# Moving a ternary quantisation and some norm sums out of a setup stage, with one multiplication given to GpSimd

## The reference

```
x = x + 0.5 * _L0_ffn_ref(_layernorm(x), w_gate_up, w_proj)     # the stage at hand
x = x + _L0_attn_ref(_layernorm(x), w_qkv, w_out)               # 16 heads
x = x + 0.5 * _L0_ffn_ref(_layernorm(x), w_gate_up, w_proj)
x = x + 0.5 * _L1_ffn_ref(...)   # mixture of experts
x = x + _L1_attn_ref(...)        # retention
x = x + 0.5 * _L1_ffn_ref(...)

def ternary_quant(w_fp32, g=64):
    w = w_fp32.astype(bfloat16); w_g = w.reshape(-1, g)
    scale = clip(mean(abs(w_g), axis=-1, keepdims=True), 1e-08, None)
    w_hat = (clip(round(w_g / scale), -1, 1) * scale).reshape(w.shape)
    return w + stop_gradient(w_hat - w)

def _L0_ffn_ref(x, w_gate_up, w_proj):      # w_gate_up [2048, 256], w_proj [256, 1024]
    gate, up = split(x @ ternary_quant(w_gate_up).T, 2)
    h = silu(gate) * up
    return rms_norm(h) @ ternary_quant(w_proj).T
```

## Time and profile before

| | us |
|---|---|
| median of 3 runs | 1762.09 (1761.56 to 1762.62) |
| profiled execution, its own time | 1760.51 |
| its span in the profile | 1758.7 |
| busy in the span: PE, DVE, ACT, POOL | 1645.4, 1287.1, 1219.9, 1126.1 |
| first matmul of the feed-forward stage begins at | 50.85 |

### The profile page before, as it was taken

How to read it: one execution, slowest core, us unless ns; L and a number is a source line. 1 busy time by engine, 2 the same in 40 slices (tenths; PEclk the granted TensorE clock), 3 DMA queues, 4 the chain that set the end, 5 groups by cost and what they waited for, 6 DMA issues and landing times.

```text
span 1758.7 us, 26693 instructions
## 1 busy us (share of the span) xinstructions
PE 1645.4 (94%) x9307; PEld 963.8 (55%) x9307; DVE 1287.1 (73%) x2427; ACT 1219.9 (69%) x1886; POOL 1126.1 (64%) x747
## 2 busy tenths in 40 slices
PE   0898789999999999999999999998999999899998
PEld 0565345555555555555555555554565565676565
DVE  7877657777777777767777777786687778886766
ACT  6655778888888888988988888874654443325432
POOL 0554768888888888888888878883763222653222
PEclk9999899999999999999999999999999999999999
DMA  8100567887888878889878788784001210000001
GB/s 284 49 1 19 101 115 144 139 138 144 150 150 146 147 140 154 148 135 164 144 136 152 130 145 151 128 137 89 0 1 58 64 40 1 1 1 28 28 10 48
DMA packets 580506, 174.03 MB, mean 99 GB/s; under 512 B 543243, under 2 KB 579350, under 8 KB 580246
## 3 DMA queue, kind: packets, MB, share of 16 engines
q1 hardware_dynamic: 580374, 172.33, 51.8%
HBM read 35.94 MB, written 2.10 MB: 22 GB/s over the span
## 4 chain that ended last, share of the span: by engine, by line
PE 73%; DVE 8%; POOL 2%; issue 2%; ACT 1%; SPq 0%; DMA 0%; DVEq 0%; POOLq 0%; ACTq 0%
PE banks L1789 23%; PE banks L1790 23%; PE banks L1791 23%; DVE X L1644 1%; POOL sq_sum L684 1%; DVE mo_h L1631 1%; DVE nmax L1463 1%; DVE x L1196 1%; PE banks L1887 1%; PE banks L1855 1%; PE banks L1888 1%; PE banks L1856 1%; PE banks L1939 0%; PE banks L1799 0%; PE banks L2100 0%
## 5 line engine op out<-in xcount | busy, mean ns | idle before, releaser
L737 POOL TENSOR_TENSOR Pl<-Pm,Ph 128x1024 f16<-128x1024 f32 x256 | 546.4, 2134 | 52.3 <-ACT Ph L962 51.3
L952 ACT ACTIVATE Pm<-banks,nbias,s_scale 128x1024 f32<-128x1024 f32 x256 | 308.0, 1203 | 135.9 <-DVE nbias L1465 135.7
L1463 DVE TENSOR_REDUCE nmax<-banks 128x1 f32<-128x1024 f32 x256 | 312.6, 1221 | 111.6 <-PE banks L1791 110.5
L962 ACT ACTIVATE Ph<-Pm 128x1024 f16<-128x1024 f32 x256 | 268.3, 1048 | 1.2
L716 POOL TENSOR_TENSOR rp_b<-rp_s,rope 128x512 f32<-128x512 f32 x128 | 162.8, 1272 | 150.9 <-ACT rp_s L929 150.9
L1502 DVE SCALAR_TENSOR_TENSOR X<-banks,rinv,X 128x256 f32<-128x256 f32 x256 | 112.7, 479 | 156.8 <-PE banks L1791 156.8
L790 POOL TENSOR_TENSOR mT_lo<-mo_h,mT_hi 128x512 f16<-128x512 f32 x72 | 83.7, 1162 | 214.2 <-ACT mT_hi L1064 213.9
L1789 PE MATMUL banks<-QK_hi 128*128 128x512 f16 x512 | 197.1, 385 | 6.8 <-DVE QK_lo L1539 2.7
L1789 PE MATMUL banks<-PT_hi,V_hi 128*128 128x512 f16 x512 | 194.9, 381 | 3.2 <-DMA PT_lo<-Pl 3.2
L1790 PE MATMUL banks<-QK_lo,QK_hi 128*128 128x512 f16 x512 | 195.5, 382 | 0.0
L1791 PE MATMUL banks<-QK_hi,QK_lo 128*128 128x512 f16 x512 | 195.5, 382 | 0.0
(11 more groups left out here) (240 smaller groups left out, 4136.4 us busy)
## 6 DMA issues: line engine op xcount, KB each, us to landing
moe_raw<-in_L_ffn_W SPq DMA_DIRECT2D x72, 128.0 KB, 2.3
w_all<-in_L_attn_w_qkv SPq DMA_DIRECT2D x3, 2048.0 KB, 16.5
a_raw<-in_L_attn_w_qkv SPq DMA_DIRECT2D x24, 256.0 KB, 3.1
PT_hi<-Ph SPq DMA_TRANSPOSE x256, 3.4
PT_lo<-Pl SPq DMA_TRANSPOSE x256, 3.4
raw_gu<-in_L_ffn_w_gate_up SPq DMA_DIRECT2D x2, 1024.0 KB, 7.3
X<-in_L_attn_x SPq DMA_DIRECT2D x2, 1024.0 KB, 13.1
o_raw<-in_L_attn_w_out SPq DMA_DIRECT2D x8, 256.0 KB, 3.4
```

What stands on the lines that cost most here:

```text
L737: nc.gpsimd.tensor_tensor(Pl[:, z % 4, :], Pm[:, k, :], Ph[:, z % 4, :], ALU.subtract).then_inc(pl_done.sem, 1)
L952: nc.scalar.activation(Pm[:, k, :], two_banks[z % 2][:], ACT.Exp, bias=nbias[:, z:z + 1], scale=s_scale[:], accum_out=rsum[:, z:z + 1]).th ...
L962: nc.scalar.activation(Ph[:, z % 4, :], Pm[:, (base * SLOTS + z) % 3, :], copy).then_inc(ph_done.sem, 1)
L1463: nc.vector.tensor_reduce(nmax[:, z:z + 1], two_banks[z % 2][:], AX, ALU.max, negate=True).then_inc(max_done.sem, 1)
```

## The change

In the setup DVE no longer makes `size` and `signed`. POOL multiplies the signs by the scales (`signed_scale`), and DVE multiplies that by the mask (`quantised`). Part 2 (the down weights) is summed and scaled in the setup as before, but its mask, `quantised`, difference and straight through run at ht 0 to 3 of phase 0 on DVE; its transposes run on PE behind `up(4)` to `up(7)`, and their evictions on DVE and ACT. The squares of the value weights (`w_all` 2) move to ACT in phase 1, in four pieces; the norm's sum, root and scales to phases 2 and 3; the split of the gate weights (`gate_weights_split`) from phase 0 to phase 3. The three big weight DMAs are issued ahead of the four small constants. Buffers are laid out anew, so that part 2 survives into phase 0.

```diff
+        WP_AFTER = {4: 0, 5: 1, 6: 2, 7: 3}
...
         @block.sync
+            for i in range(2):
+                sp.dma_start(of_part(raw, i).rearrange("p (r g) k -> p r (g k)", r=FT),
+                             w_gu[i * FF:(i + 1) * FF].rearrange("(r p) d -> p r d", p=P)).then_inc(w_in[i].sem, 16)
+            sp.dma_start(raw[1][:].rearrange("p (r g) k -> p r (g k)", r=DC),
+                         w_proj.rearrange("(r p) h -> p r h", p=P)).then_inc(w_in[2].sem, 16)
             sp.dma_start(ident[:], t_ident).then_inc(consts_in.sem, 16)
...
-            sp.wait_ge(w_squared.sem, 4)
+            sp.wait_ge(w_squared.sem, 3 + SQ_PIECES)
         @block.gpsimd
+            def signed_scale(i):
+                pool.wait_ge(quant_step[i].sem, 3)
+                pool.wait_ge(w_sign[i].sem, 1)
+                sign, scale = of_part(q_sign, i), of_part(q_scale2, i)
+                nc.gpsimd.tensor_tensor(sign, sign, scale.unsqueeze(2).broadcast_to([P, scale.shape[1], GROUP]), ALU.mult).then_inc(w_signed[i].sem, 1)
+            signed_scale(0)
             rsqrt_ln(0, 0, 0)
-            pool.wait_ge(w_norm_made.sem, 1)
-            nc.gpsimd.tensor_tensor(w_root[:], w_norm[:], neg_half[:, 0:4], ALU.pow).then_inc(w_root_made.sem, 1)
+            signed_scale(1)
+            signed_scale(2)
         @block.scalar
+            sign_of(0)
+            sign_of(1)
+            bf16_of(0)
+            bf16_of(1)
+            sign_of(2)
+            bf16_of(2)
...
-            for m in range(3):
+            for m in range(2):
                 act.wait_ge(w_all_in[m].sem, 16)
                 nc.scalar.activation(w_all[m][:], w_all[m][:], ACT.Square, accum_out=w_sq[:, m:m + 1]).then_inc(w_squared.sem, 1)
...
+                    if f == 0 and s - 1 in WP_AFTER and WP_AFTER[s - 1] % 2:
+                        down_weights(WP_AFTER[s - 1])
+                    if f == 0 and phase == 1 and ht in (2, 3, 4, 5):
+                        value_weights_squared(ht - 2)
         @block.vector
+            mask(0)
             dve.wait_ge(x_in[0].sem, 16)
             for t in range(TPH):
                 ln_statistics(0, 0, t)
             ln_variance(0, 0, 0)
...
+            mask(1)
+            ln_normalise(0, 0, 0)
+            for i in range(2):
+                quantised(i)
+                difference(i)
+                straight_through(i)
             ln_lo(0, 0, 0)
...
+                    if f == 0 and phase == 0 and ht < 4:
+                        (mask, quantised, difference, straight_through)[ht](2)
+                    if f == 0 and s - 1 in WP_AFTER and WP_AFTER[s - 1] % 2 == 0:
+                        down_weights(WP_AFTER[s - 1])
...
+                    if f == 0 and phase == 3 and ht == 2:
+                        scales()
+                    if f == 0 and phase == 3 and ht == 5:
                         gate_weights_split()
         @block.tensor
+                    if f == 0 and s in WP_AFTER:
+                        down_weights(WP_AFTER[s])
+                    if (f, s) == (0, FT):
+                        pe.wait_ge(setup_copied.sem, N_SETUP_ACT)
+                        pe.wait_ge(setup_copied_v.sem, N_SETUP_V)
```

More of the change, by code:

```diff
@@ L125, in build_program @@
     rstd = sb("rstd", [P, B, TT], f32)
-    w_sq = sb("w_sq", [P, 4], f32)
+    w_sq = sb("w_sq", [P, 4 + SQ_PIECES], f32)
+    identb = sb("identb", [P, P], bf16)
+    ones_all = sb("ones_all", [P, P], f32)
     w_norm = sb("w_norm", [P, 4], f32)
@@ L162, in build_program @@
     place["at"] = phase0
[L163 to L185, removed]
     ff_s = sb("ff_s", [P, 2, HALF], f32)
     ff_h = sb("ff_h", [P, 3, HALF], f32)
+    hT_at = place["at"]
     hT_hi = sb("hT_hi", [P, NHALF, FT, HALF], f32r)
+    hT_lo_at = place["at"]
     hT_lo = sb("hT_lo", [P, NHALF, FT, HALF], f32r)
+    sq_at = place["at"]
     ff_sq = sb("ff_sq", [P, 2, HALF], f32)
@@ L1226, in _ @@
             ln_variance(0, 0, 0)
[L1228 to L1232, removed]
-                nc.vector.tensor_tensor(part(i, 0, q_size), part(i, 5, q_mask), over_groups(part(i, 0, q_scale2)),
-                                        ALU.mult).then_inc(quant_step[i].sem, 1)
-            def signed(i):
-                dve.wait_ge(w_sign[i].sem, 1)
-                nc.vector.tensor_tensor(part(i, 0, q_what), part(i, 6, q_size), part(i, 0, q_sign), ALU.mult).then_inc(quant_step[i].sem, 1)
@@ L1240, in difference @@
-            def difference(i):
-                dve.wait_ge(w_bf16[i].sem, 1)
-                nc.vector.tensor_tensor(part(i, 0, q_diff), part(i, 7, q_what), part(i, 0, q_w), ALU.subtract).then_inc(quant_step[i].sem, 1)
-            def straight_through(i):
-                nc.vector.tensor_tensor(part(i, 0, q_out), part(i, 0, q_w), part(i, 8, q_diff), ALU.add).then_inc(quant_step[i].sem, 1)
-            for i in range(len(QUANT)):
-                mask(i)
-                if i == 0:
-                    ln_normalise(0, 0, 0)
@@ L1252, in _ @@
-            ln_lo(0, 0, 0)
-            for stage in (size, signed):
-                for i in range(len(QUANT)):
-                    stage(i)
-            for i in range(2):
-                difference(i)
-            for i in range(2):
-                straight_through(i)
-            difference(2)
-            straight_through(2)
-            dve.wait_ge(w_norm_psum.sem, 1)
-            nc.vector.tensor_scalar(w_norm[:], bank[5][:, 0:4], 1e-30, None, ALU.max).then_inc(w_norm_made.sem, 1)
-            for i in range(0, N_WP, 2):
+            mask(1)
@@ L1900, in ffn @@
                             pe.wait_ge(l_step.sem, 5)
+                        if not f and phase == 2:
+                            pe.wait_ge(w_norm_made.sem, 1)
                         transpose_x(1, l, phase - 1)
```

138 lines of the change are left out of this document (95 added, 43 removed).

## The result

| | before | changed |
|---|---|---|
| median of seven runs each, us | 1761.56 (1759.53 to 1762.62) | 1771.67 (1768.09 to 1774.72) |
| ratio, 95% interval | | 1.0058 [1.0048, 1.0068] |
| span of the profiled execution, us | 1758.7 | 1768.1 |
| first feed-forward matmul, us | 50.85 | 49.41 |
| step 9 begins behind step 0, us | 19.1 | 29.0 |

The kernel became 0.58% slower: 10.1 us by the medians, 9.4 by the spans of the two profiled executions. The last four rows of the table add up to the second figure, to rounding: -1.4 + 9.9 + 1.5 - 0.5.

A forecast was written before the change was run, and what follows sets the result against it. It took the setup as bound by DVE, phase 0 as full on DVE and the rest as at PE's pace. Start 1.2, clock 1.3, phase 0 7.0 and later phases 0.7 made 10.2 us; 1762.1 + 10.2 = 1772, range 1762 to 1778.

The forecast's parts named there:

- a sum of 10.2: Whole kernel: start 1.2, clock 1.3, phase 0 7.0 and later phases 0.7 make it 10.2 us slower.
- DVE and POOL take turns: Setup and phase 0: operations reading two SBUF tensors, and `XN`, alternate between the engines; `mask(0)` held until 21.2 us.
- The multiplication, 4.2 us: Setup: each 128x2048 multiplication on POOL takes 4.2 us, bounds 2.1 to 6.
- the 36.9: Setup: if the last `XN` ends by 36.9 us, the stage starts no later than before; 38.1 was forecast.
- ACT as the new bound of the setup: Setup: ACT's squares and evictions, behind `XN`, end at 52.0 us; the stage starts 1.2 us later than before.
- the signs: What would show it right: `mask(0)` over 6 us, ACT's `w_all` squares not before 40, step 9 26 us behind step 0.
- The clock at the start, 1.3 us: Stage start: the first 3 to 4 us of PE run at 1.2 GHz, costing 1.3 us.
- Phase 0, 7.0 us: Phase 0: the work moved onto full DVE delays PE; step 9 starts 26.1 us behind step 0, not 19.1.
- a rival (with 5 us): Setup or phase 0: a 6 us multiplication, or a second clock fall during PE's wait; 5 us more, 1777; 12%.
- Later phases, 0.7 us: Behind phase 0: value squares, the norm's matmul and `gate_weights_split` in phase 3 together cost 0.7 us.
- Without exclusion: Setup, rival: POOL's multiplications don't hold DVE's bf16 operations; stage starts 11.4 us earlier, sum -3.9, 1758; 11%.
- A short multiplication: Setup, rival: 2.1 us on POOL, sum 3.9, 1766; shares its 15% with phase 0 losing 3 rather than 7.

The follow-up runs named there:

- e2: The changed kernel with POOL waiting for all four `XN` ahead of its second multiplication; 1766.54 us, ratio 1.0033.
- e7: The kernel before with only POOL's three multiplications of signs by scales in place of DVE's `size` and `signed`; 1765.90 us, ratio 1.0017.
- e6: The changed kernel with extra matmuls that nobody reads filling two of PE's waits, in the setup and behind step 4; 1767.83 us, ratio 1.0038.
- e3: The changed kernel with the four quantisation operations of part 2 on DVE ahead of step 0; 1764.26 us, ratio 1.0010.
- e5: The kernel of e10 with the chain of scales and the gate split also moved to phase 3; 1761.22 us, ratio 0.9994.
- e10: The kernel before with only the three weight loads issued ahead of the four small constants; 1760.74 us, ratio 0.9986.
- e1: The changed kernel with the multiplications of signs by scales back on DVE, none on POOL; 1769.30 us, ratio 1.0040.
- e4: The changed kernel with the transposes and evictions of the down weights two steps later; 1766.56 us, ratio 1.0033.
- e8: The changed kernel with the edits of e2 and e3 together; 1762.78 us, ratio 0.9999.

## Why the prediction was right, and where it was not

The direction, the mechanism and the size held: 1772 us predicted, 1771.67 measured. By the profiled pair it was 9.4 us against a sum of 10.2, and three of the sum's four terms were off, one of them against the other two.

- **DVE and POOL take turns.** Right, also for bf16, which no row of before showed. e2, e7 and the 7.95 us of `XN` show it. It reaches further than assumed: `mask(0)` wasn't the instruction that was held (2.28 us, where over 6 was given as a sign), the three thresholds ahead of it were, which have 32 columns and one tensor input. A row of before had shown as much: `gwT_hi`, 16 columns, takes 1.24 us beside two adds of POOL that last from 65.10 to 68.04. The prediction counted that hold where the row stands and didn't carry it over to the thresholds.
- **The multiplication, 4.2 us.** Mis-sized: 3.60 to 3.65. It was extrapolated from float32 rows of 512 and 1024 columns; of the bounds, 2.1 to 6, it lies near the middle. Three of them stand ahead of `XN`, so the last `XN` ends at 36.1 instead of 38.1. That is below the 36.9 under which, by the prediction's own working, the stage starts no later than before.
- **ACT as the new bound of the setup.** Right, with squares at 37.97 and 41.56 (not before 40, said the signs), and evictions from 45.36. But with `XN` 2 us sooner, the start is 49.4, 1.4 us ahead of before, where 1.2 behind was predicted. The term was +1.2 and measured -1.4; the multiplications explain about 1.8 of the 2.6, allowances between `XN`, squares and evictions the rest.
- **The clock at the start, 1.3 us.** About right: the first matmuls are 0.43 us apart as predicted, and the steps 0 to 5 take 1.8 us more than with a busy PE (e6).
- **Phase 0, 7.0 us.** The walk through DVE's list put step 5 at 16.4 us behind step 0, with the clock's 1.3 at 17.7. It began 17.7 behind (67.15 less 49.41). e3 shows that these four steps on DVE's queue in phase 0 are what costs. The error is behind it: four steps at PE's pace were to take 9.7, and took 11.2, because the clock was at its lower level behind the 4.31 us of waiting. This second fall stood in a rival (with 5 us); it belonged into the sum, with 1.5. e6 measures 2.1 for the same stretch. With the clock's 1.3 counted in, 27.4 us were forecast from step 0 to step 9 (the signs say 26), and 29.0 measured.
- **Later phases, 0.7 us.** 1.5. The extra time lies between step 22 and step 26: PE waits 1.2 us in front of step 26 for an `ff_h` that stands behind `XN` of 2.89 us, with two operations of POOL beside them. POOL's `w_root` of 1.46 us now stands at 125.9, ahead of those two, and pushes them there. The prediction counted the squares and the norm's matmul, but not this operation on POOL's queue. e5 narrows it down: its scales and gate split stand in phase 3 too, but its `w_root` is still in the setup, and there the same `XN` takes 1.36 us and the piece from step 22 to step 26 is 9.3 us, as in e7 and e10, against 10.7 in the changed kernel (9.05 before). That `w_root` and not the moved squares or the norm's matmul is the cause was not tried by itself.
- **The rivals.** Without exclusion the stage would have started 11 us sooner; e7 excludes it. A short multiplication, under 3 us, is excluded by POOL's rows.

The two rows of the later phases, from the changed kernel:

```profile
125.89 1.46 POOL L732 TENSOR_TENSOR w_root<-w_norm,small 128x4 f32<-128x4 f32 x1
...
129.04 2.89 DVE L1235 TENSOR_SCALAR XN<-X,mean,rstd 128x256 f32<-128x256 f32 x4
```

So the error of the setup (-2.6) and those of phase 0 and of the later phases (+1.6 and +0.8) nearly cancelled, with another -0.5 behind the stage. The closeness of 1772 to the median is in part luck. One slip had no effect: the change doesn't take 10 us of work from DVE's list but 12, since part 2's mask, difference and straight through leave it as well and two `quantised` come in.

Where did the loss come from, by the runs? POOL's exchange costs 3.3 us in the kernel before (e7) and, in the changed one, 8.4 at the start of the stage and 4.9 up to step 9 (e1), the early weight loads give 1.8 (e10), the four quantisation steps in phase 0 with the fall of the clock behind them cost 7 (e3), and the order `XN` behind the multiplications costs about 3 to 5 (e2), part of which is e1's figure seen again. These pieces overlap and don't add up. What leaves the setup (part 2's work, one square on ACT, the scales) shows between e10 and e1, both without POOL's multiplications: a start at 41.0 for 49.0, and 13.4 us more from there to step 9. So what left the setup cost more in phase 0 than it had saved.

## What to carry to other kernels

Before work goes from DVE to POOL, put both timelines side by side: where the two take turns, an offloaded instruction costs DVE about its length on POOL (3.6 us) and saves its length on DVE (2.2), and it holds whatever stands next in DVE's list, urgent or not. Work that leaves a serial setup for a pipelined phase is hidden only if the phase has room on that engine; the 6 us of idle DVE ahead of step 0 took it nearly for free, the full steps 0 to 3 did not. And a wait on PE can have two prices, its length and the time at the lower clock behind it; an engine that was hidden (POOL's sums of squares) turns up as the next wait once the first is gone.

## What the hardware showed that was not expected

- A `tensor_tensor` of 128x2048 bf16 with a scale for each 64 columns takes 3.60 to 3.65 us on POOL and 2.28 on DVE. The same multiplication without the broadcast operand takes 1.2 on DVE.
- Even three operations of 128x32 on DVE with one input are held by POOL: 3.76 us for 0.35. But `ff_h`, which reads one tensor from PSUM, keeps its 0.68 beside POOL's sums (63.68 and 66.61 in the changed kernel).
- The clock's falls don't follow from the length of one wait: 1.83 us idle in e5 stood before 6.8 us at 1.2 GHz (a mean granted clock of 0.81 from 66 to 84 us), 1.98 us in e4, 1.84 in e8 and even 3.72 in e1, in front of step 4, before none: the matmuls behind them start 0.22 us apart. What PE did around these waits differs; which part of it decides was not tried.
- At the head of the program the column of the granted clock says 1.00 while matmuls start 0.43 us apart, so there it doesn't tell the clock.
